# Attention by sequences, retrieval with a stationary operand of 32 columns, and GpSimd's share of the one-hots, in a four-block network

## The reference

```python
# attention; H = 32 heads, D = 64, blocks of 32 tokens, a state per head
qkv = silu(x @ qkv_w.T).reshape(b, s, H, 3 * D); q, k, v = split(qkv, 3)
intra = (q_i @ k_i.T * decay) @ v_i ;  inter = (q_i * query_decay) @ state
state = state * block_decay + (k_i * key_decay).T @ v_i
out   = (sigmoid(x @ gate_w.T) * rmsnorm(intra + inter, norm_w)) @ out_w.T
# retrieval; 8 heads, 8 experts a head: 64 slots for each token
h = silu(x @ W_up.T + b_up) @ W_down.T + b_down ;  q = h @ W_q.T
scores, idx = top_k(q . keys, 8)                    # for each of two key halves, 45 keys
sc, pk = top_k(sum of all 64 pairs, 8) ;  indices = idx_x * 45 + idx_y
z = silu((h . down_embed[indices]) * softmax(sc)) ;  out = sum(z * up_embed[indices])
```

## Time and profile before

| | |
|---|---|
| median of 3 runs | 2260.09 us |
| the profiled execution | 2259.77 us, span 2257.9 us |
| mean granted TensorE clock | 0.945 |
| TensorE busy | 1976.8 us (88%), 15672 matmuls |
| loads of the stationary operand | 1607.6 us (71%) |
| VectorE busy | 1470.2 us (65%) |
| ScalarE busy | 812.2 us (36%) |
| GpSimd busy | 490.3 us (22%) |

### The profile page before, as it was taken

The page is one execution under the profiler, slowest core; times in us unless marked ns, Lnnn a source line. Parts: engine busy times, 40 slices in busy tenths (PEclk is TensorE's granted clock), DMA queues, the critical chain, the costliest instruction groups (busy, mean ns, idle before and its releaser), DMA issues. The chain is left out here.

```text
span 2257.9 us, 42613 instructions
## 1 busy us (share of the span) xinstructions
PE 1976.8 (88%) x15672; PEld 1607.6 (71%) x15672; DVE 1470.2 (65%) x3367; ACT 812.2 (36%) x1366; POOL 490.3 (22%) x457
## 2 busy tenths in 40 slices
PE   7899999999998868999974666669599999999996
PEld 5788888888886656778741222246489999999996
DVE  0045555555555546544448999945899898989974
ACT  4422322232323324444445544423243333333330
POOL 2233333333334019100003666520000000000000
PEclk9999999999999969999986988879799999999998
DMA  1100000000002033222210000030102111111101
GB/s 60 34 13 11 21 21 10 21 10 21 21 10 74 0 119 101 86 86 96 86 33 0 0 1 1 0 121 0 76 39 77 39 74 42 53 63 40 76 39 38
DMA packets 47705, 96.81 MB, mean 43 GB/s; under 512 B 10944, under 2 KB 28224, under 8 KB 44872
## 3 DMA queue, kind: packets, MB, share of 16 engines
q1 hardware_dynamic: 47484, 95.13, 12.6%
q10 hardware_dynamic: 108, 0.15, 0.0%
HBM read 92.75 MB, written 2.51 MB: 42 GB/s over the span
## 5 line engine op out<-in xcount | busy, mean ns | idle before, releaser
L1674 PEld LDWEIGHTS re_ps_wheel<-re_sb_spread,re_sb_of_b 128*128 128x128 bf16 x3072 | 216.4, 155 | 7.4 <-issue 2.1
L1674 PE MATMUL re_ps_wheel<-re_sb_spread,re_sb_of_b 128*128 128x32 bf16 x3072 | 217.2, 255 | 0.4 <-DVE re_sb_spread L1855 0.4
L1741 ACT ACTIVATE re_sb_z<-re_ps_misc 128x512 bf16<-128x512 f32 x192 | 105.8, 593 | 243.3 <-PE re_ps_misc L1621 188.2
L1664 PE MATMUL re_ps_wheel<-re_sb_z,re_sb_is_b 128*128 128x32 bf16 x3072 | 178.6, 235 | 9.9 <-DVE re_sb_is_b L1817 9.8
L1664 PEld LDWEIGHTS re_ps_wheel<-re_sb_z,re_sb_is_b 128*128 128x128 bf16 x3072 | 176.7, 115 | 10.6 <-issue 10.6
L1298 POOL TENSOR_TENSOR sc_sb_bx<-sc_sb_dtx,sc_sb_bs 128x1024 f32<-128x1024 f32 x64 | 150.5, 2353 | 84.4 <-DVE sc_sb_h L1310 70.4
L1310 DVE TENSOR_TENSOR_SCAN sc_sb_h<-sc_ps_a,sc_sb_bx 128x512 f32<-128x512 f32 x128 | 150.3, 1206 | 21.1 <-ACT sc_ps_a L1288 21.1
L1014 DVE TENSOR_TENSOR mo_sb_gated<-mo_sb_hidden,mo_sb_gate 128x512 f32<-128x512 f32 x100 | 72.8, 728 | 130.0 <-ACT mo_sb_hidden L984 129.4
L413 DVE COPY at_sb_v<-at_ps_v 128x256 f32<-128x256 f32 x128 | 53.6, 419 | 158.7 <-PE at_ps_v L296 158.7
L491 POOL TENSOR_TENSOR g_sb_squares_sum<-g_sb_squares_sum,at_sb_qT 128x512 f32<-128x512 f32 x64 | 81.7, 1277 | 346.2 <-ACT at_sb_qT L396 346.2
L294 PE MATMUL at_ps_v<-at_sb_wH,all_sb_x_part 128*128 128x256 f32 x512 | 131.1, 334 | 8.9 <-POOL at_sb_w_part L470 8.9
(11 more groups left out here) (249 smaller groups left out, 4875.1 us busy)
## 6 DMA issues: line engine op xcount, KB each, us to landing
re_sb_b_all<-re_b SPq DMA_DIRECT2D x16, 2048.0 KB, 7.4
mo_sb_gate<-mo_gates SPq DMA_DIRECT2D x36, 256.0 KB, 3.1
at_sb_w<-in_qkv_w_dram SPq DMA_DIRECT2D x17, 384.0 KB, 3.1
mo_sb_w<-in_w_dram SPq DMA_DIRECT2D x10, 640.0 KB, 9.6
mo_sb_gate<-mo_gates SPq DMA_DIRECT2D x20, 192.0 KB, 2.8
mo_sb_gate<-mo_gates SPq DMA_DIRECT2D x16, 224.0 KB, 3.0
at_sb_tbl<-in_decay_dram SPq DMA_DIRECT2D x17, 193.5 KB, 2.9
mo_sb_gate<-mo_gates SPq DMA_DIRECT2D x20, 160.0 KB, 2.6
```

The source lines that it names most:

```text
L1664: last = nc.tensor.matmul(wheels[:, q, :, t].rearrange("p (a r) -> p a r", a=2), is_b[:, token, :], z[:, n, :, :].rearrange("p r (a t) -> ...
L1674: last = nc.tensor.matmul(wheels[:, q, :, t], of_b[T % 2][q // 2][:, :, (q % 2) * QT + t], spread[:, q, n, :, t], start=(n == 0), stop=(n ...
L1741: nc.scalar.activation(z[:, n, 4 * j:4 * j + 4, :].rearrange("p a t -> p (a t)"), misc[j % 2][:, :], ACT.Copy).then_inc(S["z_ready"], 1)
```

## The change

Attention. The order of units becomes sequence by sequence: unit k is now sequence k // 2 and pair k % 2. v is projected once for both pairs of a turn: the weights of v of both pairs lie side by side (wv, 256 columns, and its parts wvH and wvL), and project_v runs only in front of the first of two units, with three matmuls of 256 columns in place of 256 + 128 for one pair. The sum in PSUM is complete, so that VectorE's sum_v goes away and ScalarE applies Silu straight from PSUM (keep_v, two operations for each half). v has three slots. The weights of q and k, of v, and the tables each have their own load and semaphore. The first loads are issued at the start of the gate phase, ahead of its own, and cut by GpSimd at its end; in each later turn the loads follow the last use, and the cuts stand in units 6 and 7. SP waits at the end for the last tables. The padding of the inputs grows by one pair. The projection phase's semaphores are cleared at its end with one barrier of its own.

Retrieval. Gather and scatter swap their operands: 32 columns (z of a token, or spread of a token) are stationary, 128 columns (is_b, or of_b of that token) stream, and four neighbouring tokens go to four groups of 32 partitions of the result (the column groups of the array). The gathered values come out transposed; ScalarE copies them to SBUF (pull), and TensorE picks each token's own rows with a constant (select, 32 fp32 matmuls of 64 by 64). After the scatter ScalarE copies the result (lift) and TensorE transposes it back (flip, 16 transposes) before copy_W. The first portion of the product stands between gather and select; the scatter is in one piece, with the scores behind it and the flips last. of_a has 16 rows in place of 32, weigh is two operations of 128 partitions in place of four of 64, spread is block-diagonal with zeros written once (memset), of_b is laid out by pairs of tokens, found is one operation whose result is written in a run, and its sum is three additions (four, two, xy). is_b is made half by VectorE and half by GpSimd.

The core of the diff, with the indentation cut:

```diff
+    load_first(sp)
...
+def load_v(sp, a):
+    for j in range(HALVES):
+        of = D["qkv_w"][ds(a + j, 1), :, :].rearrange("o p (k f) -> p (o k) f", k=KD)[:, :, 2 * P:3 * P]
+        sp.dma_start(wv[:, :, j * P:(j + 1) * P], of).then_inc(wv_loaded, 16)
...
+def load_first(sp):
+    load_v(sp, 0)
+    for j in range(HALVES):
+        load(sp, j, j)
+        load_tables(sp, j, j)
+def cut_first(pool):
+    cut_v(pool, 0)
+    for j in range(HALVES):
+        cut(pool, j, 0)
+gate_phase(nc, M, D, G, load_first, cut_first)
...
+    wait_apart(sp, q_product, done(i, UNITS - 2) - UNITS, M.passed)
+    load(sp, 0, i * HALVES + HALVES)
+    wait_apart(sp, v_product, v_done(i, BATCH - 1, 1) - UNITS, M.passed)
+    load_v(sp, i * HALVES + HALVES)
+    wait_apart(sp, q_product, done(i, UNITS - 1) - UNITS, M.passed)
+    load(sp, 1, i * HALVES + HALVES + 1)
+    wait_apart(sp, gated, done(i, UNITS - 2), M.passed)
+    load_tables(sp, 0, i * HALVES + HALVES)
+    wait_apart(sp, gated, done(i, UNITS - 1), M.passed)
+    load_tables(sp, 1, i * HALVES + HALVES + 1)
+for j in range(HALVES):
+    sp.wait_ge(t_loaded[j], (TURNS + 1) * 32)
...
+    pe.wait_ge(v_ready, v_done(i, b, half) - 1)
     for t in range(2):
         start = b * BLK + (2 * half + t) * P
+        to = ps_v[:, 2 * t * P:2 * (t + 1) * P]
         for c in range(KD):
-            nc.tensor.matmul(ps_v[:, 2 * t * P:2 * (t + 1) * P], M.xH[:, c, start:start + P],
-                             wH[j][:, c, 2 * P:4 * P], start=(c == 0), stop=False, skip_group_check=True)
-            last = nc.tensor.matmul(ps_v[:, 2 * t * P:(2 * t + 1) * P], M.xL[:, c, start:start + P],
-                                    wH[j][:, c, 2 * P:3 * P], start=False, stop=(c == KD - 1),
-                                    skip_group_check=True)
+            nc.tensor.matmul(to, M.xH[:, c, start:start + P], wvH[:, c, :], start=(c == 0), stop=False)
+            nc.tensor.matmul(to, M.xH[:, c, start:start + P], wvL[:, c, :], start=False, stop=False)
+            last = nc.tensor.matmul(to, M.xL[:, c, start:start + P], wvH[:, c, :], start=False,
+                                    stop=(c == KD - 1))
     last.then_inc(v_product, 1)
...
+if j == 0:
+    project_v(pe, i, b, 0)
...
+def keep_v(i, b, half):
+    act.wait_ge(v_product, v_done(i, b, half) - UNITS)
+    act.wait_ge(attended, done(i, HALVES * (b - 1)))
+    for j in range(HALVES):
+        last = nc.scalar.activation(v_of(b, j)[:, 2 * half:2 * half + 2, :],
+                                    ps_v[:, :].rearrange("p (t a f) -> p a t f", t=2, a=HALVES)[:, j],
+                                    ACT.Silu)
+    last.then_inc(v_ready, 1)
...
+if k == UNITS - 2:
+    cut(pool, 0, i + 1)
+    cut_v(pool, i + 1)
+if k == UNITS - 1:
+    cut(pool, 1, i + 1)
...
 def gather(T, q):
     after(pe, "z_ready", (T + 1) * 4 * PARTS)
-    after(pe, "is_b_ready", T * QUARTERS + q + 1)
+    if q < OWN_QUARTERS:
+        after(pe, "is_b_ready", T * OWN_QUARTERS + q + 1)
+    else:
+        after(pe, "is_b_pooled", T * (QUARTERS - OWN_QUARTERS) + q - OWN_QUARTERS + 1)
     after(pe, "W_ready", (T - 1) * QUARTERS + q + 1)
-    for t in range(QT):
-        token = q * QT + t
+    for j in range(q * JQ, (q + 1) * JQ):
         for n in range(PARTS):
-            last = nc.tensor.matmul(wheels[:, q, :, t].rearrange("p (a r) -> p a r", a=2),
-                                    is_b[:, token, :],
-                                    z[:, n, :, :].rearrange("p r (a t) -> p a r t", a=2)[:, :, :, token],
-                                    start=(n == 0), stop=(n == PARTS - 1))
+            for g in range(QUARTERS):
+                token = QUARTERS * j + g
+                last = nc.tensor.matmul(
+                    wheel[g * 2 * ROWS:(g + 1) * 2 * ROWS, j * P:(j + 1) * P],
+                    z[:, n, :, :, token].rearrange("p a r -> p (a r)"),
+                    is_b[:, token, :], start=(n == 0), stop=(n == PARTS - 1))
     last.then_inc(S["gathered"], 1)
+def select(T, c):
+    after(pe, "pull", T * QUARTERS + 2 * c + 2)
+    for k in range(2 * JQ):
+        j = c * 2 * JQ + k
+        for half in range(2):
+            of = slice(half * TWIN, (half + 1) * TWIN)
+            last = nc.tensor.matmul(wheel[of, c * BLK + k * TWIN:c * BLK + (k + 1) * TWIN],
+                                    pulled[:, j, of], twin[:, half, :], start=True, stop=True)
+    last.then_inc(S["selected"], 1)
 def scatter(T, q):
     after(pe, "spread_ready", T * 2 + q // 2 + 1)
-    for t in range(QT):
+    for j in range(q * JQ, (q + 1) * JQ):
         for n in range(PARTS):
-            last = nc.tensor.matmul(wheels[:, q, :, t], of_b[T % 2][q // 2][:, :, (q % 2) * QT + t],
-                                    spread[:, q, n, :, t], start=(n == 0), stop=(n == PARTS - 1))
+            for g in range(QUARTERS):
+                token = QUARTERS * j + g
+                last = nc.tensor.matmul(
+                    wheel[g * 2 * ROWS:(g + 1) * 2 * ROWS, j * P:(j + 1) * P],
+                    spread[:, n, :, token],
+                    of_b[T % 2][token // HALF_TWIN][:, token % HALF_TWIN // 2, :, token % 2],
+                    start=(n == 0), stop=(n == PARTS - 1))
     last.then_inc(S["scattered"], 1)
+def flip(T, q):
+    after(pe, "lift", T * QUARTERS + q + 1)
+    for j in range(q * JQ, (q + 1) * JQ):
+        last = nc.tensor.transpose(wheel[:, j * P:(j + 1) * P], lifted[:, j, :], M.ident[:, :])
...
+if live(I - 1):
+    product(I - 1, 0)
+if live(I):
+    select(I, 0)
+    select(I, 1)
...
+def pull(T, q):
+    after(act, "gathered", T * QUARTERS + q + 1)
+    after(act, "selected", T * 2)
+    nc.scalar.activation(pulled[:, q * JQ:(q + 1) * JQ, :].rearrange("p j k -> p (j k)"), lane(q), ACT.Copy
+                         ).then_inc(S["pull"], 1)
+def lift(T, q):
+    after(act, "scattered", T * QUARTERS + q + 1)
+    after(act, "flipped", (T - 1) * QUARTERS + q + 1)
+    nc.scalar.activation(lifted[:, q * JQ:(q + 1) * JQ, :].rearrange("p j k -> p (j k)"), lane(q), ACT.Copy
+                         ).then_inc(S["lift"], 1)
...
+@block.gpsimd
+def _(pool):
+    pool.wait_ge(tables_loaded, TABLES * 16)
+    for T in range(TILES):
+        after(pool, "b_spread", (T + 1) * 16)
+        after(pool, "gathered", T * QUARTERS)
+        for q in range(OWN_QUARTERS, QUARTERS):
+            of = slice(q * QT, (q + 1) * QT)
+            nc.gpsimd.tensor_scalar(is_b[:, of, :], b_all[:, of, :], own[:, 0:1], None, ALU.is_equal
+                                    ).then_inc(S["is_b_pooled"], 1)
...
+shape = [P, HALF_TWIN // 2, GRID, 2]
+t = slice(c * HALF_TWIN, (c + 1) * HALF_TWIN)
+nc.vector.tensor_tensor(of_b[T % 2][c][:, :, :, :], rows[:, :, :].unsqueeze(1).broadcast_to(shape),
+                        splitT[T % 2][:, 0, t].rearrange("p (t k) -> p t k", k=2).unsqueeze(2)
+                        .broadcast_to(shape), ALU.is_equal
...
+    after(dve, "selected", T * 2 + c + 1)
+    t = slice(c * HALF_TWIN, (c + 1) * HALF_TWIN)
+    nc.vector.tensor_tensor(masked[:, :, t], lane(c).rearrange("p (t a) -> p a t", a=ROWS),
+                            of_a[:, :, t], ALU.mult).then_inc(S["masked_ready"], 1)
+dve.wait_ge(S["masked_ready"], T * 2 + 2)
+then(nc.vector.tensor_reduce(zs[:, :], masked.rearrange("p a t -> p t a"), AX.X, ALU.add))
...
+then(nc.vector.tensor_tensor(found[:, :, :, :].rearrange("p a i (h k) -> p (a i) h k", h=RHEADS),
+                             hit[:, :, :, :].rearrange("p a i (h k) -> p (a i) h k", h=RHEADS),
+                             place16[:, :, :, :].rearrange("p a i h -> p (a i) h").unsqueeze(3)
+                             .broadcast_to([P, 2 * K_HEAD, RHEADS, K_HEAD]), ALU.mult))
+then(nc.vector.tensor_tensor(four[:, :, :, :], found[:, :, 0:4, :], found[:, :, 4:8, :], ALU.add))
...
+then(nc.vector.memset(spread[:, :, :, :], 0.0))
...
```

More of the change, by code:

```diff
@@ L1546, in retrieval_phase @@
         hit = s.sb("hit", [P, 2, K_HEAD, SLOTS], BF16)
-        found = s.sb("found", [P, 2, SLOTS, K_HEAD], BF16)
+        found = s.sb("found", [P, 2, K_HEAD, SLOTS], BF16)
+        four = s.sb("four", [P, 2, K_HEAD // 2, SLOTS], BF16)
+        two = s.sb("two", [P, 2, K_HEAD // 4, SLOTS], BF16)
         xy = s.sb("xy", [P, 2, SLOTS])
@@ L1699, in _ @@
                             lower_z(I + 1, part, 1)
-                        if live(I - 1):
+                        if live(I - 1) and part:
                             product(I - 1, part)
@@ L1708, in _ @@
                         lower_z(I + 1, 3, 2)
-                    for q in range(2):
-                        if live(I):
+                    if live(I):
+                        for q in range(QUARTERS):
                             scatter(I, q)
@@ L1814, in marks @@
                     after(dve, "gathered", T * QUARTERS)
-                    for q in range(QUARTERS):
+                    for q in range(OWN_QUARTERS):
                         of = slice(q * QT, (q + 1) * QT)
```

290 lines of the change are left out of this document (145 added, 145 removed).

## The result

The changed kernel takes 2142.4 us (median of 4 runs, 2142.1 to 2142.7) against 2259.7 us (median of 4): ratio 0.948, 95% interval 0.9465 to 0.9498. That is 117 us less; the forecast was 178 us less, 2082 us. The profiled execution has a span of 2140.8 us.

| from the trace, us | before | after | change | forecast |
|---|---|---|---|---|
| first matmul of the projection's product | 688.74 | 651.57 | -37.2 | -38.5 |
| from there to the first gather | 938.4 | 940.6 | +2.1 | -8 |
| 15 periods, gather to gather | 573.8 | 501.5 | -72.4 | -122 |
| last gather's start to the end | 56.9 | 47.2 | -9.7 | -8.8 |

The account below looks back on a forecast made before the run. TensorE was taken to bound the attention and retrieval loops, VectorE close behind in the retrieval. From the profiled 2259.8 us, -38.5 for the attention and -139 for the retrieval gave 2082 us, range 2050 to 2165.

Parts of the forecast that it names:

- the likeliest case (1): Retrieval: pairs at 20 to 33 ns, VectorE 28 to 31 us a tile; 2058 to 2117 us, chance 0.60.
- rival (2): Retrieval: VectorE becomes the bound, through of_b, found or GpSimd beside it; 2117 to 2182 us, chance 0.18.
- GpSimd beside VectorE: Retrieval: VectorE slowed by GpSimd working at the same time, +1 us a tile (0 to 3).
- The period: Retrieval: one tile on TensorE, gather to gather, falls from 38.56 to 30.4 us, 122 us over 15 periods.
- Ahead of the first gather: Before the retrieval's first gather VectorE is the bound; shorter look-ups, less the memset of spread, give -8 us.
- TensorE's terms: Retrieval tile: gather and scatter 5.2 us each at 27 ns a pair, select 2.1 us, flips 2.2 us.
- (3): Retrieval: one column group's weight loads wait for the others' streams; 40 ns a pair, 2158 us, chance 0.10.
- (4): Retrieval: column groups don't run side by side, pairs cost 57 and 69 ns; slower at 2297 us, chance 0.07.
- VectorE's other terms: Retrieval tile: of_b unchanged at 2.24 us each, found -4.0, weigh -2.3, its strided reduction +0.5, of_a -0.55 us.
- Attention: Attention phase in sum: -38.5 us, of which -33 us from projecting v once for both pairs of heads.
- the pause behind it: Between gate phase and attention: -8 us, the first attention matmul coming within 1 us of the gate's end.
- The clock: Start of the attention: -3 us for six at half speed; granted clock near 1 in both loops.

Follow-up runs that it names:

- experiment 1: The changed kernel with all four one-hots of b made by VectorE, none by GpSimd: 2097.5 us, ratio 0.929 to the kernel before.
- experiments 8 and 9: The changed kernel, all one-hots on VectorE, next tile's made ahead of the look-ups: 2069.3 us (9); with ScalarE's c also earlier: 2070.0 us (8).
- experiment 5: The changed kernel with twelve pairs of one column group behind each other in each quarter of gather and scatter: 2198.1 us.
- experiment 6: The kernel before with the change's attention alone, its old retrieval kept: 2225.2 us, ratio 0.986.

## Why the prediction was right and wrong

The range (2050 to 2165) held the time because it was drawn over the rivals; the likeliest case (1), at most 2117 us, did not happen. What happened is rival (2), VectorE becomes the bound, by the third of its causes, "GpSimd beside it costs over 4 us". It had 0.18 and the prices 2117 to 2182 us. That the time lies within those prices is in part luck: by the prediction's own sum this cause makes VectorE's tile 28.8 - 1 + 4.65 = 32.5 us and the time 2113 us; the rest came by the ring below.

- **GpSimd beside VectorE: the step that failed.** Put at +1 us a tile (0 to 3), from casts on GpSimd. Measured 4.65 (experiment 1). Those rows show how GpSimd suffers, not what VectorE pays, and that they vary from 0.39 to 0.93 us was a sign that one of the two engines can hold up the other. That the one-hots themselves would cost nothing beside the gather was right (5.44 us each, in the range of 3 to 7.5); what they hold up was not reckoned.
- **The period**: 33.43 us for 30.4, 45 us of the miss. Another 4.6 us are a plain slip: 38.56 us is one tile of the earlier trace rows, the mean of the 15 is 38.25. VectorE's own work was also less than read off: busy 34.6 us a period (519.03 us in 15) and not 35.8, so that TensorE led by more than 7%.
- **Ahead of the first gather**: -8 forecast, +2.1 measured. The look-ups did get shorter (found 1.22 us for 4.7), but GpSimd's first one-hots took it back; experiment 1, without them, has its first gather 6.7 us earlier.
- **The period without GpSimd** would still not have been 30.4 but 31.03, by the ring of experiments 8 and 9. This is the second step that failed: the prediction took the tile as the larger of the engines' sums (30.4 and 28.8), and a chain that goes from one engine to the other and back took longer than either. In the changed kernel, too, VectorE is busy for 31.5 of 33.43 us. Only with the one-hots moved does TensorE's own sum show, 29.0 us.
- **TensorE's terms**: pair 27 ns (measured 26 and 24), select 2.1 (2.0), flips 2.2 (1.9), all inside their ranges. Rivals (3) and (4) are out; only with the other order of experiment 5 does a pair come near (3)'s 40 ns.
- **VectorE's other terms**: of_b 4.50 us for two (4.49 before), so runs of two elements don't cost here. The Trainium skill, "Vector Engine (DVE) Microarchitecture Reference", section 5.1, cited in the prediction, gives two results a cycle where the innermost run is longer than one element. The trace agrees so far that two elements in a run keep the old rate (4096 in 2.25 us). The others: found 1.22 (1.1 forecast), the three additions 1.0 (0.9), weighing 1.3 to 1.5 (1.8), the strided reduction 1.92 (1.7), of_a 0.69 (0.67).
- **Attention**: -37.2 for -38.5, and this closeness is partly luck, since misses of both signs cancel: the gate's end +1.6 us for +3.5, the pause behind it -6.8 for -8, the loop -34.8 for -38, the end +2.6 for +3. (The +1 for one barrier more lies behind this mark and was 0.5, experiment 6.) The parts: v's 24 matmuls 2.94 us for two units (2.83), so -29 and not -33 over the phase; from its first matmul to its last product -34.8 us (562.7 to 527.9). The gate starts 4.2 us later (3.5), but ends only 1.6 us later, since its matmuls now start 0.227 us apart and not 0.232 (so in every run with the new attention); why is open. The first attention matmul follows 2.1 us behind the gate's end, not within 1:

```profile
109.84 0.38 PE L361 MATMUL at_ps_v<-at_sb_wvH,all_sb_x_part 128*128 128x256 f32 x1 [2.10 <-DVE at_ps_state_sum L479]
...
643.70 5.26 PE L729 MATMUL pr_ps_sum<-g_sb_squares_sum,g_sb_ones 128*128 128x512 f32 x8 [5.05 <-PEq L335]
```

- **The clock** still fell, at 111 us, behind that shorter pause of 2.1 us: the granted clock is 0.50 from 112.5 to 114.2 us (the 1.2 GHz level), and matmuls of 512 columns start 0.43 us apart until 114.2 us, where that lasted until 121 us before. It gives 1.5 us and not 3. At the end the projection waits 5.05 us where it was 2.48, 2.6 us more and not 3.

## What to carry to other kernels

Before work is moved from VectorE to GpSimd, list which VectorE instructions will stand beside it. Here those with two operands in SBUF, and some casts, waited for most of a GpSimd instruction, so that 1.35 us saved cost 4.65. If it must be, cut GpSimd's work into short instructions (the cost fell to about 1.3 us) or place it beside searches and reductions, which kept their times. Where two engines are both near 90% busy, follow the ring from one to the other and back, and issue first what the other engine waits for: that was worth 28 us with no instruction removed. Small matmuls in different column groups ran side by side here, also when they weren't direct neighbours (25 ns a pair with three in a row in one group, 45 with twelve).
